# Select stage: a batch's output rows are spread in two halves inside the next batch's score groups, and its first scores stand around the output projection

## The chip, the cores and the metric

One core of a Trainium2 chip runs the whole program. The metric is the device time of one execution in microseconds (us). TensorE (PE) multiplies matrices into PSUM, which has eight banks; VectorE (DVE) and ScalarE (ACT) read PSUM and work on tiles in SBUF; SyncE (SP) issues the DMAs. Each engine works through its own list of instructions in order and waits for semaphores that the others raise.

## What is computed

The reference is a chain of four layers over x of shape (8, 512, 256), all in float32: a mixer, a layer of experts, a delta-rule attention, and last the layer that the change touches. Of each batch's 512 tokens that layer keeps the 256 with the largest gate, lets these attend to one another with 16 heads of 16, and adds the result, times the gate, to the kept tokens:

```python
x = x + _L1_ffn_ref(_layernorm(x, axis=-1), ...)

def _L1_ffn_ref(token_inputs, Wg, Wq, Wk, Wv, Wo):
    B, N, D = token_inputs.shape          # 8, 512, 256
    C = int(N * 0.5); H = 16; dh = 16
    gate = jax.nn.sigmoid((token_inputs @ Wg)[..., 0])
    _, idx = jax.lax.top_k(gate, C)
    attn_in = jnp.take_along_axis(token_inputs, idx[..., None], axis=1)
    q, k, v = (attn_in @ W reshaped to (B, C, H, dh) for Wq, Wk, Wv)
    scores = jnp.einsum('bqhd,bkhd->bhqk', q, k) / jnp.sqrt(jnp.float32(dh))
    attn = jax.nn.softmax(scores, axis=-1)
    o = jnp.einsum('bhqk,bkhd->bqhd', attn, v).reshape(B, C, D) @ Wo
    gate_sel = jnp.take_along_axis(gate, idx, axis=1)
    out = jnp.zeros_like(token_inputs)
    return out.at[jnp.arange(B)[:, None], idx].set(o * gate_sel[..., None])
```

## The kernel before

The four layers are four stages one after the other; `stage_select` is the last, and the change lies in it alone. It runs eight batches in a pipeline of two. A loop over steps (a, b) does the attention of batch a and, between its parts, the gate, the selection and the projections of batch b = a + 1. In the first step there is only b = 0, in the last only a = 7, so there are seven joint steps. The order on each engine is written out by hand, and nothing but the order of the calls in the loops and the waits in the functions decides it.

On TensorE a joint step is, by the names of its functions and the lines that the profile gives their matmuls:

- `scores(a, 0)` (L2161): the scores of heads 0 to 3, in two halves, into banks 0, 1 and 2, 3. VectorE takes the largest of each row (`maxima`, L2396), one instruction for each half.
- `turn_h(b)` (L2199): the normed tokens of batch b turned, into banks 6 and 7; ScalarE copies them to `hT` (L2332).
- `max_rows(a, 0)` (L2170): the maxima turned into bank 4; VectorE adds them to q (`add_max`, L2401, writes `q2`).
- `gate(b)` (L2205), then `scores_turned(a, 0)` (L2178), then `gate_column(b)` (L2211). ScalarE takes the sigmoid (L2334, with a table load before and after it) and then the exponentials (L2324). VectorE copies the gate's column (L2421) and compares it with all gates, two tiles of 128 tokens by two instructions each (`ranks(b, 0, 2)`, L2406 and L2407).
- `scores(a, 1)`, `max_rows(a, 1)`, `scores_turned(a, 1)`, `values(a, 0)` (L2188), `scores(a, 2)`. Meanwhile VectorE does `maxima(a, 1)`, `add_max(a, 1)`, `ranks(b, 2, 4)`, the sum `rank` (L2428) and `psel` (L2432), the matrix of zeros and ones that picks the rows.
- `select(b)` (L2218), which needs `psel`, and `turn_select`; groups 2 and 3 of the heads; the projections of q, k (L2234) and v (L2242) of batch b; `turn_back(a)` (L2250).
- the tail: `turn_out(a)` (L2257, bank 2), `project_out(a)` (L2264, bank 3), each behind a wait for ScalarE's copy of the one before (`OT`, L2357, and `o2`, L2359), and `spread_back(a)` (L2272), eight matmuls that put the 256 rows back to their 512 places in banks 4 and 5. VectorE multiplies these by the gate, adds the tokens and writes `outb` (L2458, four instructions), then raises `fin`.

Batch b's own `scores(b, 0)` opens the next step, so it stands on TensorE behind `spread_back(a)`, and VectorE's first `maxima` of the next step stand behind the four instructions of `outb`. `max_rows(a, 0)` waits for `fin`, since it writes bank 4. SyncE waits for `fin`, issues the store of `outb` and then the load of `xin` for three batches on (L2139, L2141). `layer_norm(b + 1)` on VectorE stands ahead of `turn_back`'s reader, late in the step. The program opens the next step's work with these two functions on TensorE:

```python
for a, b in steps:
    if a is not None:
        scores(a, 0)
    if b is not None:
        turn_h(b)
    if a is not None:
        max_rows(a, 0)
```

Of the kernel before, what the change touches and what calls it, by code (L numbers as in the profile page):

```python
# [10 lines left out]
ALU = mybir.AluOpType  # L11
# [2053 lines left out]
def stage_select(nc, io, x_in, x_out):  # L2065
# [9 lines left out]
    with ctx:  # L2075
# [17 lines left out]
        gcol = sb("gcol", [P, 2, TT])  # L2093
# [23 lines left out]
                 "sp mx mtp q2 stp ex val ox otp on oTp oT o2p o2 outp fin dvA dvB dvC").split()  # L2117
# [7 lines left out]
        rows = lambda i: slice(i * PAD, (i + 1) * PAD)  # L2125

# [18 lines left out]
        def _(pe):  # L2145
# [3 lines left out]
            def scores(a, n):  # L2149
                if n == 0:  # L2150
                    pe.wait_ge(s["kT"], 2 * a + 2)
                    if a:
                        pe.wait_ge(s["on"], a)
                        pe.wait_ge(s["oT"], a)
                        pe.wait_ge(s["o2"], a)
                for half in (0, 1):
                    if n:
                        pe.wait_ge(s["ex"], a * PAIRS + 2 * n - 1 + half)
                    for j in range(ST_):
                        for i in (2 * half, 2 * half + 1):  # L2160
                            m = pe.matmul(ps[:, i, j * SEL:(j + 1) * SEL], qT[rows(i), a % 2, n, j * P:(j + 1) * P], kT[rows(i), a % 2, n, :],  # L2161
                                          start=True, stop=True, skip_group_check=True)
                    m.then_inc(s["sp"], 1)
# [104 lines left out]
            def spread_back(a):  # L2268
                pe.wait_ge(s["o2"], a + 1)
                for t in range(TT):  # L2270
                    for j in range(ST_):
                        m = pe.matmul(ps[:, 4 + t // 2, t % 2 * DIM:(t % 2 + 1) * DIM], pselT[:, a % 2, j, t * P:(t + 1) * P], o2[:, j, :],  # L2272
                                      start=(j == 0), stop=(j == ST_ - 1))
                m.then_inc(s["outp"], 1)

            for a, b in steps:
                if a is not None:
                    scores(a, 0)
                if b is not None:
                    turn_h(b)  # L2280
                if a is not None:
# [7 lines left out]
                if a is not None:  # L2289
                    scores(a, 1), max_rows(a, 1), scores_turned(a, 1), values(a, 0), scores(a, 2)  # L2290
# [20 lines left out]
                if a is not None:  # L2311
                    turn_out(a), project_out(a), spread_back(a)
# [55 lines left out]
        def _(dve):  # L2368
# [4 lines left out]
            fin = Chain(dve, s["dvC"], 1)  # L2373
# [29 lines left out]
            def ranks(b, t0, t1):  # L2403
                g = gcol[:, b % 2, :]
# [8 lines left out]

            layer_norm(0)
            for a, b in steps:
                if a is not None:
                    maxima(a, 0), add_max(a, 0)
                if b is not None:
                    place.start(b)
                    dve.wait_ge(s["gcp"], b + 1)  # L2420
                    dve.tensor_copy(gcol[:, b % 2, :], ps[:, 7, :].rearrange("p (t c) -> p t c", c=P)[:, :, 0]).then_inc(s["gc"], 1)  # L2421
# [23 lines left out]
                if a is not None:  # L2445
                    fin.start(a)
                    dve.wait_ge(s["otp"], a + 1)
                    both = ps[:, 0:2, :].rearrange("p j (h x) -> p j h x", x=PAD)
                    fin(dve.reciprocal(rec[:, :, :], both[:, :, :, DH]))
# [4 lines left out]
                    dve.wait_ge(s["outp"], a + 1)  # L2454
                    if a:
                        dve.wait_ge(s["stored"], 16 * a)
                    for t in range(TT):
                        m = dve.scalar_tensor_tensor(out=outb[:, t, :], in0=ps[:, 4 + t // 2, t % 2 * DIM:(t % 2 + 1) * DIM],  # L2458
                                                     scalar=gcol[:, a % 2, t:t + 1], in1=xin[:, a % 3, t, :], op0=ALU.mult, op1=ALU.add)
                    m.then_inc(s["fin"], 1)  # L2460
                    fin.end()
# [101 lines left out]
```

## Time and profile before

| | us |
|---|---|
| median of 3 runs | 3530.76 |
| lowest, highest | 3529.91, 3532.61 |
| the profiled execution | 3537.61 |
| its span in the profile | 3535.8 |
| one cycle of the select stage (five alike, 3209.3 to 3482.2) | 54.6 |

The profile comes from one execution, 6.85 us longer than the median. Over the whole span TensorE is busy 83% and VectorE 67%, but the four stages have different limits. The select stage takes the last 488 us, from 3047.9 on. The page's lists by line are ruled by the other stages, so the stage is read from the chain of waits, from the instructions in order of time, and from windows on single stretches of it.

### The profile page before, as it was taken

The page shows a single profiled execution, that of the slowest core. Times are in us where ns is not written, and L with a number is a line of the kernel's source. Part 1 is how long each engine was busy: PE and PEld are TensorE (multiplying, and loading weights), DVE is VectorE, ACT ScalarE, POOL GpSimd, SP SyncE. Part 2 cuts the span into 40 slices and gives each one's busy share as a digit, 9 for nine tenths or more (in the row PEclk, how much of TensorE's full clock was granted, in tenths as well). Part 3 has the DMA queues.
Part 4 walks back from the last instruction along what each step waited for, and adds up shares of the span by engine and source line. Part 5 has one row for each costly group of instructions (what it writes and reads, how often), then busy time and mean ns, then how long its engine had stood idle before and what let it go on. Part 6 is the DMA issues. An engine that isn't in the chain of part 4 may idle for free. (4 is left out here: it accounts for less than half of the span.)

```text
span 3535.8 us, 47712 instructions
## 1 busy us (share of the span) xinstructions
PE 2945.4 (83%) x17546; PEld 2205.0 (62%) x17546; DVE 2386.3 (67%) x5793; ACT 1273.9 (36%) x2465; POOL 189.5 (5%) x181
## 2 busy tenths in 40 slices
PE   5999955988999999994579797977979787488887
PEld 2656632554699999991346576665757677355554
DVE  6877723455477777777578788788878784354542
ACT  2343311221244444441344534444453542033332
POOL 0000000003301110110000000000000000000000
PEclk8999976999999999996789999999999996599988
DMA  2000054002399999975201111111111100100000
GB/s 67 12 24 18 7 132 52 12 6 108 122 324 321 317 317 322 320 279 186 83 25 47 57 40 40 37 37 37 40 34 61 46 19 1 63 13 25 13 19 13
DMA packets 203643, 326.78 MB, mean 92 GB/s; under 512 B 37449, under 2 KB 157522, under 8 KB 202258
## 3 DMA queue, kind: packets, MB, share of 16 engines
q1 hardware_dynamic: 196930, 305.97, 26.2%
q0 software_dynamic: 6480, 17.77, 1.3%
q8 instruction: 139, 2.28, 0.3%
q14 instruction: 94, 0.77, 0.1%
HBM read 275.18 MB, written 48.50 MB: 92 GB/s over the span
## 5 line engine op out<-in xcount | busy, mean ns | idle before, releaser
L767 PE MATMUL ex_ps<-ex_xbT,ex_w 128*128 128x128 f32 x4544 | 530.6, 275 | 0.6 <-issue 0.5
L767 PEld LDWEIGHTS ex_ps<-ex_xbT,ex_w 128*128 128x128 f32 x4544 | 524.1, 192 | 4.6 <-issue 0.7
L896 ACT ACTIVATE ex_t<-ex_ps,ex_b 128x128 f32<-128x128 f32 x568 | 208.8, 368 | 334.8 <-PE ex_ps L767 307.8
L1386 PE MATMUL de_ps<-de_hT,de_w 128*128 128x512 f32 x640 | 308.2, 626 | 23.2 <-DMA de_w<-in_w_kqv_dram 18.2
L711 PE MATMUL ex_ps<-ex_xT,ex_w 128*128 128x512 f32 x512 | 230.6, 607 | 12.4 <-DVE ex_gl L1008 9.1
L1386 PEld LDWEIGHTS de_ps<-de_hT,de_w 128*128 128x128 f32 x640 | 122.5, 202 | 151.0 <-issue 143.1
L1008 DVE SCALAR_TENSOR_TENSOR ex_gl<-ex_ps,ex_b,ex_t 128x128 f32<-128x128 f32 (+1 forms) x316 | 123.6, 391 | 137.0 <-ACT ex_t L896 67.5
L711 PEld LDWEIGHTS ex_ps<-ex_xT,ex_w 128*128 128x128 f32 x512 | 98.0, 195 | 131.8 <-issue 114.9
L1583 PE MATMUL de_ps<-de_qx,de_kx 128*128 128x128 f32 x512 | 77.5, 317 | 120.9 <-ACT de_qx L1650 120.9
L1583 PEld LDWEIGHTS de_ps<-de_qx,de_kx 128*128 128x128 f32 x512 | 72.1, 226 | 142.3 <-ACT de_qx L1650 122.8
L1831 DVE SCALAR_TENSOR_TENSOR de_ya<-de_kx,de_taps,de_ya 128x512 f32<-128x512 f32 x192 | 143.5, 749 | 15.8 <-ACT de_ya L1638 11.3
L1008 DVE SCALAR_TENSOR_TENSOR ex_gm<-ex_ps,ex_b,ex_t 128x128 f32<-128x128 f32 (+1 forms) x316 | 121.6, 385 | 47.5 <-ACT ex_t L869 45.4
L177 PE MATMUL mx_ps<-mx_hT,mx_w_in 128*128 128x512 f32 x320 | 143.6, 605 | 8.3 <-ACT mx_hT L249 8.3
L1831 DVE SCALAR_TENSOR_TENSOR de_ya<-de_qx,de_taps,de_ya 128x512 f32<-128x512 f32 x192 | 141.4, 750 | 7.0 <-ACT de_ya L1638 2.2
L779 PE MATMUL ex_ps<-ex_w,ex_hid 128*128 128x256 f32 x568 | 134.5, 380 | 1.8 <-DVE ex_hid L1033 1.8
L869 ACT ACTIVATE ex_t<-ex_ps,ex_b 128x512 f32<-128x512 f32 x64 | 44.0, 687 | 207.5 <-PE ex_ps L711 191.7
L211 PE MATMUL mx_ps<-mx_h2T,mx_w_fc 128*128 128x512 f32 x256 | 113.6, 603 | 0.8 <-ACT mx_h2T L271 0.8
L1030 DVE SCALAR_TENSOR_TENSOR ex_gl<-ex_gl,ex_gm 128x128 f32<-128x128 f32 (+1 forms) x316 | 105.3, 333 | 11.1 <-DVE ex_gl L1028 0.2
L1033 DVE TENSOR_TENSOR ex_hid<-ex_gl,ex_gs 128x128 f32<-128x128 f32 (+1 forms) x316 | 104.9, 332 | 11.2
L220 PE MATMUL mx_ps<-mx_w_proj,mx_hid 128*128 128x256 f32 x512 | 111.8, 379 | 0.0
L177 PEld LDWEIGHTS mx_ps<-mx_hT,mx_w_in 128*128 128x128 f32 x320 | 60.7, 193 | 81.6 <-issue 67.4
L779 PEld LDWEIGHTS ex_ps<-ex_w,ex_hid 128*128 128x128 f32 x568 | 102.5, 190 | 12.9 <-DVE ex_hid L1033 1.9
(382 smaller groups left out, 5655.9 us busy)
## 6 DMA issues: line engine op xcount, KB each, us to landing
ex_w<-in_w_all_dram SPq DMA_DIRECT2D x144, 1024.0 KB, 6.2
ex_w<-in_w_all_dram SPq DMA_DIRECT2D x72, 512.0 KB, 8.5
de_w<-in_w_kqv_dram SPq DMA_DIRECT2D x80, 256.0 KB, 3.5
de_ab<-alpha_d SPq DMA_DIRECT2D x8, 2048.0 KB, 7.2
ex_xb<-ex_xs_d SPq DMA_DIRECT2D x71, 129.0 KB
ex_xs_d<-ex_blank SPq DMA_DIRECT2D x71, 128.5 KB, 7.9
ex_w<-ex_y_d SPq DMA_DIRECT2D x16, 512.0 KB, 6.2
mx_xin<-in_x_dram SPq DMA_DIRECT2D x8, 512.0 KB, 3.9
```

The costliest lines, as they stand in the source:

```text
L177: m = pe.matmul(ps[:, (n + 2) % 4, :], w_in[:, k, part * DIM + half * P:part * DIM + (half + 1) * P], hT[:, k, :], start=(k == 0), stop=(k ...
L211: m = pe.matmul(ps[:, 4 + f % 2, :], w_fc[:, k, f * P:(f + 1) * P], h2T[:, k, :], start=(k == 0), stop=(k == KT - 1))
L220: m = pe.matmul(ps[:, 6 + t // 2, t % 2 * DIM:(t % 2 + 1) * DIM], hid[:, f, t * P:(t + 1) * P], w_proj[:, f, :], start=(f == 0), stop=(f = ...
L711: m = pe.matmul(ps[:, bank, :], w[:, k, part * HID + c * P:part * HID + (c + 1) * P], xT[:, i % (LAG + 1), k, :], start=(k == 0), stop=(k ...
L767: m = pe.matmul(ps[:, n % 4, x * BLK:(x + 1) * BLK], w[:, k, part * HID + c * P:part * HID + (c + 1) * P], xbT[sx][:, k, :], start=(k == 0 ...
L779: m = pe.matmul(ps[:, 4 + sx, t * DIM:(t + 1) * DIM], hid[:, sx, c, t * P:(t + 1) * P], w2[s][:, c, :], start=(c == 0), stop=(c == HT - 1))
L896: act.activation(t1[:, n % 2, 0:BLK], ps[:, n % 4, 0:BLK], ACT.Identity, bias=b13[s][:, 0, n:n + 1]).then_inc(t1_ready, 1)
L1008: dve.scalar_tensor_tensor(out=out[:, 0:width], in0=in0, scalar=b3[:, 1, n:n + 1], in1=t1[:, n % 2, 0:width], op0=ALU.add, op1=ALU.mult).t ...
L1030: link2(dve.scalar_tensor_tensor(out=gl[:, 0:width], in0=gl[:, 0:width], scalar=1.0, in1=gm[:, 0:width], op0=ALU.add, op1=ALU.mult))
L1386: m = pe.matmul(ps[:, n % 2, :], w[:, g % SLOTS, k, n % 2 * P:(n % 2 + 1) * P], hT[:, k, :], start=(k == 0), stop=(k == KT - 1))
L1583: m = pe.matmul(wide(pair(c))[:, hd, :], kc(b, hd, c), qc(hd, c), start=True, stop=True, skip_group_check=True)
L1831: m = dve.scalar_tensor_tensor(out=y, in0=xp(b, n)[:, i:i + SEQ], scalar=taps[:, col_of(n), i:i + 1], in1=y, op0=ALU.mult, op1=ALU.add)
```

## The change

`spread_back` gets a second argument, the part, and does two of the four tiles in each call. For batch a - 1 both parts are done in the step of batch a, part 0 ahead of `max_rows(a, 0)` and part 1 between `scores(a, 1)` and `max_rows(a, 1)`, both into bank 5. Part 1 waits until VectorE has read part 0 (`outd`). On VectorE the four instructions that write `outb` are split in two by the new `put_back`, which follows `add_max(a, 0)` and `add_max(a, 1)`. `fin` is raised after part 1, and the wait for it moves from `max_rows(a, 0)` to `max_rows(a, 2)`, the first to write bank 5. `gcol` is kept for three batches instead of two. The last batch's two parts follow the loop, in banks 4 and 5.

`scores(b, 0)` is cut into its halves. The first stands between `turn_out(a)` and `project_out(a)` and waits for k and for `on` (banks 0 and 1 read). The second stands behind `project_out(a)` and `turn_h(b + 1)` and waits for `oT` and `o2` (banks 2 and 3 read). `turn_h(b + 1)` itself moves from the next step to this place. No arithmetic is added or left out.

```diff
+        spread_bank = lambda a, part: 4 if a == BATCH - 1 and part == 0 else 5
...
+            def first_scores(a, half):
+                if half == 0:
                     pe.wait_ge(s["kT"], 2 * a + 2)
                     if a:
                         pe.wait_ge(s["on"], a)
-                        pe.wait_ge(s["oT"], a)
-                        pe.wait_ge(s["o2"], a)
+                elif a:
+                    pe.wait_ge(s["oT"], a)
+                    pe.wait_ge(s["o2"], a)
+                score_half(a, 0, half)
...
             def max_rows(a, n):
                 pe.wait_ge(s["mx"], a * PAIRS + 2 * n + 2)
-                if n == 0 and a:
+                if n == 2 and a:
                     pe.wait_ge(s["fin"], a)
...
-            def spread_back(a):
+            def spread_back(a, part):
                 pe.wait_ge(s["o2"], a + 1)
-                for t in range(TT):
+                if part and spread_bank(a, 0) == spread_bank(a, 1):
+                    pe.wait_ge(s["outd"], a + 1)
+                for t in (2 * part, 2 * part + 1):
...
             for a, b in steps:
-                if a is not None:
-                    scores(a, 0)
-                if b is not None:
+                if a is None:
                     turn_h(b)
-                if a is not None:
+                else:
+                    if a:
+                        spread_back(a - 1, 0)
                     max_rows(a, 0)
...
-                    scores(a, 1), max_rows(a, 1), scores_turned(a, 1), values(a, 0), scores(a, 2)
+                    scores(a, 1)
+                    if a:
+                        spread_back(a - 1, 1)
+                    max_rows(a, 1), scores_turned(a, 1), values(a, 0), scores(a, 2)
...
-                    turn_out(a), project_out(a), spread_back(a)
+                    turn_out(a)
+                if b is not None:
+                    first_scores(b, 0)
+                if a is not None:
+                    project_out(a)
+                if b is not None:
+                    if b + 1 < BATCH:
+                        turn_h(b + 1)
+                    first_scores(b, 1)
+            spread_back(BATCH - 1, 0), spread_back(BATCH - 1, 1)
...
+            def put_back(a, part):
+                if part == 0:
+                    if a:
+                        dve.wait_ge(s["stored"], 16 * a)
+                dve.wait_ge(s["outp"], 2 * a + part + 1)
+                for t in (2 * part, 2 * part + 1):
+                    m = dve.scalar_tensor_tensor(out=outb[:, t, :], ...)
+                m.then_inc(s["fin"] if part else s["outd"], 1)
...
                 if a is not None:
                     maxima(a, 0), add_max(a, 0)
+                    if a:
+                        put_back(a - 1, 0)
...
                     maxima(a, 1), add_max(a, 1)
+                    if a:
+                        put_back(a - 1, 1)
```

On TensorE, from the end of the first joint step into the second, before (each row one kind of matmul in a row, the last number how many):

```order
950 L2257 MATMUL se_ps<-se_ident,se_O 128x128 x4
951 L2264 MATMUL se_ps<-se_wo,se_OT 128x256 x4
952 L2272 MATMUL se_ps<-se_o,se_pselT 128x256 x8
953 L2161 MATMUL se_ps<-se_kT,se_qT 128x256 x8
954 L2199 MATMUL se_ps<-se_ident,se_h 128x128 x8
955 L2170 MATMUL se_ps<-se_ident,se_M 128x128 x2
956 L2205 MATMUL se_ps<-se_hT,se_wg 128x512 x2
957 L2178 MATMUL se_ps<-se_q,se_kT 128x256 x8
958 L2211 MATMUL se_ps<-se_ident,se_gb 128x128 x4
959 L2161 MATMUL se_ps<-se_kT,se_qT 128x256 x8
960 L2170 MATMUL se_ps<-se_ident,se_M 128x128 x2
```

And now, where L2153 are scores, L2271 the output projection, L2206 `turn_h`, L2281 the spreading and L2177 `max_rows`:

```order
951 L2264 MATMUL se_ps<-se_ident,se_O 128x128 x4
952 L2153 MATMUL se_ps<-se_kT,se_qT 128x256 x4
953 L2271 MATMUL se_ps<-se_wo,se_OT 128x256 x4
954 L2206 MATMUL se_ps<-se_ident,se_h 128x128 x8
955 L2153 MATMUL se_ps<-se_kT,se_qT 128x256 x4
956 L2281 MATMUL se_ps<-se_o,se_pselT 128x256 x4
957 L2177 MATMUL se_ps<-se_ident,se_M 128x128 x2
958 L2212 MATMUL se_ps<-se_hT,se_wg 128x512 x2
959 L2185 MATMUL se_ps<-se_q,se_kT 128x256 x8
960 L2218 MATMUL se_ps<-se_ident,se_gb 128x128 x4
961 L2153 MATMUL se_ps<-se_kT,se_qT 128x256 x8
962 L2281 MATMUL se_ps<-se_o,se_pselT 128x256 x4
```

Four of the eight spreading matmuls are gone from in front of L2177, and stand behind the second group's scores; the first scores are now ahead of both.

On VectorE, at the end of the program, where only the last batch's attention runs, the two halves of the seventh batch stand between that batch's groups (L2417 maxima, L2422 `add_max`, L2441 `put_back`):

```order
4632 L2441 SCALAR_TENSOR_TENSOR se_outb<-se_ps,se_gcol,se_xin 128x256 x2
4633 L2417 TENSOR_REDUCE se_M<-se_ps 128x2x2 x2
4634 L2422 TENSOR_TENSOR se_q<-se_qT,se_ps 128x256
4635 L2441 SCALAR_TENSOR_TENSOR se_outb<-se_ps,se_gcol,se_xin 128x256 x2
4636 L2417 TENSOR_REDUCE se_M<-se_ps 128x2x2 x2
```

Before, all four (L2458) stood ahead of the first maxima; in a joint step the same pairs stand ahead of the gate's column and ahead of `ranks(b, 2, 4)`.

## Rows read from the trace of the kernel before

**Rows 1.** Windows on one whole cycle: length, busy time by engine, granted clock last-but-two.

```profile
core 0: us, PE busy (x) PEld busy (x) DVE busy (x) ACT busy (x) POOL busy (x), PEclk, DMA share, GB/s
3318.40:3373.00 54.60, 44.92 (x318) 30.83 (x317) 27.47 (x69) 17.82 (x21) 0.00 (x0) 0.91 0.06 20
```

**Rows 2.** The chain that ended last, tail and head of a cycle: start, length.

```profile
3364.91 2.01 PE se_ps L2264 x8
3367.59 3.73 PE se_ps L2272 x16
3371.34 1.66 DVE se_outb L2458 x4
3373.00 2.27 DVE se_M L2396 x2
...
3381.81 0.77 DVE se_cmp L2407 x2
3384.19 2.37 DVE se_M L2396 x2
...
3393.65 3.65 PE se_ps L2218 x16
```

**Rows 3.** In order of time, tail of a cycle: start, length, engine, line, idle before.

```profile
3363.57 0.60 PE L2257 MATMUL se_ps<-se_ident,se_O 128*128 128x128 f32 x4
...
3364.26 0.59 ACT L2357 ACTIVATE se_OT<-se_ps 128x512 f32<-128x512 f32 x1
...
3366.94 0.60 ACT L2359 ACTIVATE se_o<-se_ps 128x512 f32<-128x512 f32 x1 [2.08 <-PE se_ps L2264]
...
3371.24 1.16 PE L2161 MATMUL se_ps<-se_kT,se_qT 32*128 32x256 f32 x16
...
3372.33 1.09 PE L2199 MATMUL se_ps<-se_ident,se_h 128*128 128x128 f32 x8
```

**Rows 4.** In order of time, head of the cycle before, up to the next layer norm.

```profile
3320.72 0.44 PE L2170 MATMUL se_ps<-se_ident,se_M 128*128 128x128 f32 x2 [1.90 <-DVE se_M L2396]
...
3326.22 0.16 DVE L2421 COPY se_gcol<-se_ps 128x4 f32<-128x4 f32 x1 [4.61 <-PE se_ps L2211]
...
3332.00 0.69 PE L2170 MATMUL se_ps<-se_ident,se_M 128*128 128x128 f32 x2 [2.82 <-DVE se_M L2396]
...
3332.72 0.42 DVE L2401 TENSOR_TENSOR se_q<-se_qT,se_ps 128x256 f32<-128x256 f32 x1 [0.78 <-PE se_ps L2170]
3333.06 0.74 DVE L2406 TENSOR_SCALAR_CACHE_REDUCE se_cmp<-se_gb,se_gcol 128x512 f32<-128x512 f32 x1
...
3336.42 1.14 DVE L2432 TENSOR_SCALAR se_psel<-se_iota,se_rank 128x256 f32<-128x256 f32 x4
...
3338.97 3.72 PE L2218 MATMUL se_ps<-se_psel,se_h 128*128 128x256 f32 x16
...
3351.12 1.40 DVE L2379 BATCH_NORM_STATS2 se_stats<-se_xin 128x6 f32<-128x256 f32 x4
```

**Rows 5.** Windows on stretches of that cycle: the clock that TensorE was granted.

```profile
3321.60:3324.80 3.20, 3.20 (x11) 1.12 (x14) 0.01 (x1) 0.64 (x2) 0.00 (x0) 0.50 0.38 130
3328.30:3331.70 3.40, 0.88 (x8) 0.43 (x6) 3.33 (x6) 0.00 (x0) 0.00 (x0) 1.00 0.00 0
3331.80:3338.50 6.70, 5.99 (x46) 3.56 (x50) 4.80 (x15) 1.94 (x2) 0.00 (x0) 0.50 0.01 2
3338.60:3372.60 34.00, 30.50 (x226) 22.66 (x221) 14.18 (x40) 9.75 (x13) 0.00 (x0) 1.00 0.00 0
```

**Rows 6.** In order of time, the same head in the first joint step, at full clock.

```profile
3104.30 0.44 PE L2170 MATMUL se_ps<-se_ident,se_M 128*128 128x128 f32 x2 [1.41 <-DVE se_M L2396]
...
3108.17 0.16 DVE L2421 COPY se_gcol<-se_ps 128x4 f32<-128x4 f32 x1 [2.97 <-PE se_ps L2211]
```

**Rows 7.** The tile `se_xin` on SyncE's queue: time from issue to landing.

```profile
DMA to landing us min/median/max: 3.8/4.6/10.1
```

**Rows 8.** In order of time, the last step: its second `max_rows`.

```profile
3493.22 0.69 PE L2170 MATMUL se_ps<-se_ident,se_M 128*128 128x128 f32 x2 [1.55 <-DVE se_M L2396]
```

More of the change, by code:

```diff
@@ L2092, in stage_select @@
         gb = sb("gb", [P, SEQ])
-        gcol = sb("gcol", [P, 2, TT])
+        gcol = sb("gcol", [P, 3, TT])
         cmp = sb("cmp", [P, SEQ])
@@ L2147, in _, with score_half @@
             pe.wait_ge(s["zeroed"], 3)
-            def scores(a, n):
-                if n == 0:
+            def score_half(a, n, half):
+                for j in range(ST_):
+                    for i in (2 * half, 2 * half + 1):
+                        m = pe.matmul(ps[:, i, j * SEL:(j + 1) * SEL], qT[rows(i), a % 2, n, j * P:(j + 1) * P], kT[rows(i), a % 2, n, :],
+                                      start=True, stop=True, skip_group_check=True)
+                m.then_inc(s["sp"], 1)
+            def first_scores(a, half):
+                if half == 0:
                     pe.wait_ge(s["kT"], 2 * a + 2)
@@ L2153, in scores @@
                         pe.wait_ge(s["on"], a)
-                        pe.wait_ge(s["oT"], a)
-                        pe.wait_ge(s["o2"], a)
-                for half in (0, 1):
[L2157 to L2163, printed above, removed]
+                elif a:
+                    pe.wait_ge(s["oT"], a)
+                    pe.wait_ge(s["o2"], a)
+                score_half(a, 0, half)
+            def scores(a, n):
+                for half in (0, 1):
+                    pe.wait_ge(s["ex"], a * PAIRS + 2 * n - 1 + half)
+                    score_half(a, n, half)
             def max_rows(a, n):
                 pe.wait_ge(s["mx"], a * PAIRS + 2 * n + 2)
-                if n == 0 and a:
+                if n == 2 and a:
                     pe.wait_ge(s["fin"], a)
@@ L2372, in _ @@
             place = Chain(dve, s["dvB"], 9)
-            fin = Chain(dve, s["dvC"], 1)
+            div = Chain(dve, s["dvC"], 1)
             def layer_norm(b):
@@ L2412, in picked @@
                 dve.tensor_copy(pselT[:, b % 2, j, :], ps[:, 7 - j, :]).then_inc(s["pT"], 1)
+            def put_back(a, part):
[4 more added lines that the diff above has]
+                for t in (2 * part, 2 * part + 1):
+                    m = dve.scalar_tensor_tensor(out=outb[:, t, :], in0=ps[:, spread_bank(a, part), t % 2 * DIM:(t % 2 + 1) * DIM],
+                                                 scalar=gcol[:, a % 3, t:t + 1], in1=xin[:, a % 3, t, :], op0=ALU.mult, op1=ALU.add)
+                m.then_inc(s["fin"] if part else s["outd"], 1)
             layer_norm(0)
@@ L2453, in _ @@
                     m.then_inc(s["on"], 1)
[L2454 to L2461, printed above, removed]
+                    div.end()
+            put_back(BATCH - 1, 0), put_back(BATCH - 1, 1)
     return own
```

12 lines of the change are left out of this document (6 added, 6 removed).

## The prediction

> **What bounds the kernel now.** I read the windows by cycle first, then the chain of waits, then the instructions in order of time, then windows on the clock. The page's lists by line are no help here, since the stage that changes is the last seventh of the span. A cycle of the select stage takes 54.60 us [rows 1], with TensorE busy 44.9 and VectorE 27.5. Neither is full, so the length is set by a chain that changes engines. The chain in [rows 2] shows which one. In the tail it is the output projection (3364.91), the spreading (3367.59, 3.73 us), the four instructions of `outb` on VectorE (3371.34, 1.66) and only then the first maxima (3373.00, 2.27). The scores which these maxima read were made at 3371.24 and had waited for nothing but TensorE's order [rows 3]. In the head the chain runs over the compares (L2407) to the second maxima at 3384.19, and over TensorE from there to `select` at 3393.65. Behind `select` TensorE is busy 30.5 of 34.0 us [rows 5] and is itself the bound. The change goes at the tail and touches the head.
>
> I cut the cycle at five points and ask of each piece how long it is now and how long it will be. The pieces are taken from the cycle 3318.40 to 3373.00. Its repetition is exact enough to carry points over: `outb` starts at 3371.34, and the second `max_rows` of this cycle, 3332.00, lies where the chain's maxima of the next cycle (3384.19 + 2.37 = 3386.56) place it one period of 54.60 later. So the next first `max_rows` is at 3320.72 + 54.60 = 3375.32.
>
> **Piece A, from the end of `turn_out` to the first `max_rows`.** Now: 3363.57 + 0.60 = 3364.17 [rows 3] to 3375.32, that is 11.15 us. After the change TensorE does, from 3364.17:
> - the first half of the scores, half of 1.16 us, taken as 0.55. It ends at 3364.72. ScalarE's `OT` is ready only at 3364.26 + 0.59 = 3364.85, so this half costs nothing: it fills a wait.
> - the output projection from 3364.91 as now, 1.99 us, to 3366.90.
> - `turn_h`, 1.09 us, to 3367.97. ScalarE's `o2` (3366.94 + 0.60) is done within it, so the wait of 0.7 us ahead of the spreading is covered as well.
> - the second half of the scores, 0.55, to 3368.5, and half of the spreading, 1.83 (half of 3.73 less the overlap of neighbours), to 3370.35.
> The first maxima now run beside this: the first half during the output projection, the second from 3368.5 to 3369.7 (half of 2.37). They are ready before TensorE is, so `max_rows` starts at 3370.35. The piece is 6.18 long and gives back 4.97 us. Taken apart these are the second half of the spreading, 1.83, `outb` 1.66 off the chain, and the rest of the maxima's wait.
>
> **Piece B, first `max_rows` to the gate's column.** Now 3320.72 to 3326.22, 5.50 us [rows 4]. In the first joint step the same instructions take 3104.30 to 3108.17, 3.87 us [rows 6]. The difference is the clock: from 3321.60 to 3324.80 the granted clock is 0.50, the 1.2 GHz level [rows 5], after TensorE had sat idle 1.90 us ahead of `max_rows` [rows 4]. Piece A leaves TensorE without a gap there, so I expect full clock and 1.63 us back. `put_back` of part 0 (half of 1.66, 0.83) stands on VectorE between `add_max` and the gate's column. It waits for a spreading that is already done, and VectorE was idle 4.61 us there [rows 4]. It costs nothing. Queued behind it are the column and the compares, for which TensorE's second maxima wait; the cover lasts as long as part 0 ends 2 us before the column.
>
> **Piece C, gate's column to the second `max_rows`.** Now 3326.22 to 3332.00, 5.78 us, and VectorE is busy through it (compares, then maxima). It stays. The spreading's second part goes into TensorE's wait of 2.82 us there [rows 4], and at full clock its 1.83 fits with about 1.2 us to spare, since the scores are done at about 2.75 us after the column and the maxima at 5.78. At the low clock it takes 3.65 and overshoots by some 1.2 us.
>
> **Piece D, second `max_rows` to `select`.** Now 3332.00 to 3338.97, 6.97 us, set by TensorE at clock 0.50 from 3331.80 to 3338.50 [rows 5]; `psel` was done at 3336.42 + 1.14 = 3337.56, 1.4 us earlier. Afterwards VectorE sets it: `max_rows` 0.44, `add_max` 0.42 with two hand-overs of 0.05, `put_back` of part 1 at 0.83, then compares to `psel` as now, 3333.06 to 3337.56, 4.50. Together 6.26. That gives back 0.71. Were it not for `put_back` it would give 1.5, so 0.83 of the moved work is paid here.
>
> **Piece E, `select` to the end of `turn_out`,** 3338.97 to 3364.17, 25.2 us at full clock, has nothing changed in it. The new wait for `fin` in the third group is for something finished some 7 us earlier.
>
> **SyncE.** The load of `xin` for three batches on now follows `fin` in the step in which its layer norm comes. Part 1 is put back about 1.7 us after the second `max_rows`, issue of store and load takes 0.9, the transfer lands 4.6 us later (at most 10.1) [rows 7]. The layer norm starts 3351.12 - 3332.00 = 19.1 us after that `max_rows` [rows 4]. So 12 us are left, 6 in the worst case. Cost nothing.
>
> **The clock's share.** A, B and D give 4.97 + 1.63 + 0.71 = 7.3 us, a cycle of 47.3, if TensorE keeps the full clock. It may not. In the new cycle it waits about 1.2 us ahead of the second group's scores, 1.2 ahead of the second `max_rows` and 2.2 ahead of `select`. In the trace, waits of 1.90 and 2.82 us in otherwise thin stretches (0.88 busy of 3.40, 3328.30 to 3331.70) were followed by half clock for 3.2 us or 6.7 us [rows 4, 5]. A half-clock stretch like the short one that falls on `select`, where TensorE is the bound, costs half of its length, 1.6 us. Bounds are none (0) and two in each cycle (3.2). By the nearest row, the 1.90 us wait with one short stretch behind it, I take one in each cycle and a second in a few: 2.0 us.
>
> The Trainium skill (TensorE: Matmul & The Clock Gate, HAM oscillation — how this bites in real kernels) tells of a kernel whose bursts of matmuls each start at the low clock because the engine idles between them. [...]
>
> **The sum.** Piece A occurs in seven tails. Six are as above, 6 × 4.97 = 29.8; in the last there is no `turn_h`, so the wait for `o2` shows again, while today's piece is as long: 5.4. B and D occur in six steps: 9.8 and 4.3. That is 49.3 us at full clock. The clock takes back 7 × 2.0 = 14.0. In the last step part 1 of the seventh batch stands in a wait of 1.55 us [rows 8] and needs 1.83 to 3.65; the final `outb` now overlaps the spreading by 0.83. Net a loss of 0.7. In all 34.6 us. Against the profiled execution: 3537.6 - 34.6 = 3503.0. The median of the runs lies 6.85 below the profiled execution, so 3496.
>
> **Rivals.**
> 1. The clock holds through every cycle. For it: the new cycle has fewer and shorter gaps. Against it: 2.2 us of wait ahead of `select`. Saves 50: 3481.
> 2. Two half-clock stretches in every cycle, one of them on the spreading's second part, which then overshoots and delays `max_rows`. For it: thin work from the gate's column to `select`. Saves 49.3 - 7 × 3.2 - 1.3 = 25.6: 3505.
> 3. Slower. TensorE's clock falls ahead of `select` and does not come back through piece E, where TensorE is the bound, so every microsecond at half clock costs half a microsecond. It eats the 7.3 us of a cycle once 14.6 us more are at half clock, and is slower by over 0.2% (7 us) from 16.6; at 20 us per cycle it is 3530.8 + 7 × 2.7 = 3550. Against it: in the cycle before, the clock was back within 6.8 us each time, and `select` has 3.7 us of unbroken work [rows 4, 5].
> 4. It doesn't do what it says: the maxima's second half or the new order still waits for something that I have missed, such as `put_back` holding up the column, and the tail's gain is paid in the head. Saves 0 to 7: 3528.
>
> **How the numbers follow.** Forecast (3488 to 3502) 0.62; rival 1 0.12; rival 2 0.17; rival 3 0.03; rival 4 0.03; something between 2 and 4, 0.03. The range 3484 to 3507 holds the forecast, nearly all of rival 2 and the slower edge of rival 1, about 0.8. A difference under 0.2% can't be told from none in this kernel. Faster 0.94, same 0.03, slower 0.03.
>
> **What the profile would show.** A: no `outb` ahead of the first maxima, half of the scores ahead of the output projection, TensorE without a gap over 0.3 us from `turn_out` to the gate. B: 3.9 us from `max_rows` to the column. C: still 5.8, with four spreading matmuls in it. D: 6.3, with `select` waiting for `psel`. Cycles of 47.3 to 51, and the granted clock at 0.50 for one short stretch near `select`. Wrong would be: cycles over 52, TensorE waiting for `outp`'s reader, or the layer norm waiting for its DMA.

## The result and the profile after

The changed kernel takes 3484.95 us (median of four runs, 3477.10 to 3488.47), against 3530.34 for the kernel before: a ratio of 0.9868 with a 95% interval of 0.985 to 0.9887. The forecast was 3496. The kernel is faster, as forecast, but by 45 us instead of 35.

The page of the profiled execution, which itself took 3488.47 us, begins so (engine, busy us and share, instructions):

```profile
span 3486.7 us, 47719 instructions
PE 2929.8 (84%) x17546; PEld 2202.5 (63%) x17546; DVE 2386.9 (68%) x5793; ACT 1273.2 (37%) x2465; POOL 187.2 (5%) x181
```

TensorE does the same 17546 matmuls. The windows on whole cycles, from one `select` to the next, answer to [rows 1] and, by their clock, to [rows 5]; the last one is the last step from its first `max_rows` on:

```profile
core 0: us, PE busy (x) PEld busy (x) DVE busy (x) ACT busy (x) POOL busy (x), PEclk, DMA share, GB/s
3215.23:3262.86 47.63, 42.20 (x317) 30.08 (x317) 27.48 (x69) 17.81 (x21) 0.00 (x0) 1.00 0.08 23
3358.10:3405.73 47.63, 42.20 (x316) 30.07 (x316) 27.48 (x69) 17.81 (x21) 0.00 (x0) 1.00 0.04 12
3437.59:3486.70 49.11, 33.94 (x229) 21.12 (x227) 13.20 (x21) 9.97 (x11) 0.00 (x0) 0.79 0.07 22
```

The six cycles between the second `select` and the eighth, which I call the steady ones, are all 47.6 us long, and the granted clock is 1.00 in each, where it was 0.91. VectorE's and ScalarE's work per cycle is as before (27.5 and 17.8); TensorE's busy time has fallen from 44.9 to 42.2, although it does the same matmuls, chiefly because none of them runs at half clock.

The instructions of one cycle in order of time answer to [rows 3, 4]. L2153 are scores, L2271 the output projection, L2206 `turn_h`, L2281 the spreading, L2177 `max_rows`, L2212 the gate, L2225 `select`:

```profile
3287.45 0.60 PE L2264 MATMUL se_ps<-se_ident,se_O 128*128 128x128 f32 x4
...
3287.98 1.13 PE L2153 MATMUL se_ps<-se_kT,se_qT 32*128 32x256 f32 x8
...
3289.04 2.00 PE L2271 MATMUL se_ps<-se_wo,se_OT 128*128 128x256 f32 x8
3289.16 1.23 DVE L2417 TENSOR_REDUCE se_M<-se_ps 128x4 f32<-128x1024 f32 x1 [2.09 <-PE se_ps L2153]
...
3290.87 1.04 PE L2206 MATMUL se_ps<-se_ident,se_h 128*128 128x128 f32 x8
...
3291.84 1.13 PE L2153 MATMUL se_ps<-se_kT,se_qT 32*128 32x256 f32 x8
...
3292.90 2.00 PE L2281 MATMUL se_ps<-se_o,se_pselT 128*128 128x256 f32 x8
...
3294.73 0.38 PE L2177 MATMUL se_ps<-se_ident,se_M 128*128 128x128 f32 x2
...
3294.95 1.88 PE L2212 MATMUL se_ps<-se_hT,se_wg 128*128 128x512 f32 x4
...
3298.55 0.16 DVE L2454 COPY se_gcol<-se_ps 128x4 f32<-128x4 f32 x1 [2.19 <-PE se_ps L2218]
...
3301.83 2.00 PE L2281 MATMUL se_ps<-se_o,se_pselT 128*128 128x256 f32 x8
...
3304.32 0.44 PE L2177 MATMUL se_ps<-se_ident,se_M 128*128 128x128 f32 x2 [0.50 <-DVE se_M L2417]
...
3305.14 0.87 DVE L2441 SCALAR_TENSOR_TENSOR se_outb<-se_ps,se_gcol,se_xin 128x256 f32<-128x256 f32 x2
...
3306.46 1.94 ACT L2345 ACTIVATE se_PT<-se_ps 128x1024 f32<-128x1024 f32 x2 [5.74 <-PE se_ps L2185]
...
3307.53 2.05 PE L2153 MATMUL se_ps<-se_kT,se_qT 32*128 32x256 f32 x16
...
3310.48 3.72 PE L2225 MATMUL se_ps<-se_psel,se_h 128*128 128x256 f32 x16 [0.90 <-DVE se_psel L2467]
```

TensorE goes from `turn_out` to the gate's column without a gap. The second half of the spreading stands in the wait ahead of the second `max_rows`, of which 0.50 us is left (2.82 before). `select` waits 0.90 us for `psel`.

### Where the 49 us between the two profiled executions lie

| stretch | before | after | saved |
|---|---|---|---|
| up to the first `select` (earlier stages and the first batch) | 3084.45 | 3083.11 | 1.3 |
| first `select` to the second | 36.27 | 36.86 | -0.6 |
| second `select` to the eighth, six cycles | 327.47 | 285.76 | 41.7 |
| eighth `select` to the end | 87.61 | 80.97 | 6.6 |

Before rounding the sum is 49.1, which is also the difference of the executions, 3537.61 and 3488.47.

**How the runs are compared.** The first `select` starts at another time in each profile, although nothing ahead of it differs between the kernels: from 3067 to 3090 us over the thirteen profiles. Three profiles taken on one chip, e9 to e11, already differ by 19 us there. So a run's time carries some 20 us from the earlier stages. That the execution with the profile lay 6.85 us above the median of before may come from there too, but no profile of a median run shows it. Below, besides the runs, I give **the stage**: from the start of the first `select` to the end of the span. It is 451.4 us before and 403.6 after. It is read from one execution for each kernel.

### The profile page after: what moved, and what is told of

The parts are those of the page before. It is cut to its first block and busy times, and to the rows that moved or that the text cites. A ratio compares the mean times of both kernels' runs of the same rounds, so it can differ in the third digit from the quotient of the medians.

```text
span 3486.7 us, 47719 instructions
## 1 busy us (share of the span) xinstructions
PE 2929.8 (84%) x17546; PEld 2202.5 (63%) x17546; DVE 2386.9 (68%) x5793; ACT 1273.2 (37%) x2465; POOL 187.2 (5%) x181
## 5 line engine op out<-in xcount | busy, mean ns | idle before, releaser
L1008 DVE SCALAR_TENSOR_TENSOR ex_gm<-ex_ps,ex_b,ex_t 128x128 f32<-128x128 f32 (+1 forms) x316 | 121.8, 385 | 48.1 <-ACT ex_t L869 46.8
L2417 DVE TENSOR_REDUCE se_M<-se_ps 128x4 f32<-128x1024 f32 x64 | 76.2, 1222 | 70.3 <-PE se_ps L2153 70.1
```

What stands on the lines that cost most here:

```text
L1008: dve.scalar_tensor_tensor(out=out[:, 0:width], in0=in0, scalar=b3[:, 1, n:n + 1], in1=t1[:, n % 2, 0:width], op0=ALU.add, op1=ALU.mult).t ...
L2417: dve.tensor_reduce(M[:, n, :, at].rearrange("p j i -> p i j"), ps[:, 2 * half:2 * half + 2, :].rearrange("p i (j n) -> p i j n", n=SEL), ...
```

## The experiments

My theory after the result: the pieces A, B and D of the prediction are right in mechanism and nearly in size, and the term for the clock was too high, because the changed order leaves no wait long enough. Its rival: the clock is a matter of chance in each execution, and the profiled one was lucky. Each experiment ran four to eleven times against the kernel before. e1 to e4 shared one chip and their runs of before, e5 to e8 a second and e9 to e11 a third. The columns on cycles and the stage come from one profile for each kernel.

| kernel | median | ratio to before, interval | cycles | stage |
|---|---|---|---|---|
| before | 3530.34 | | 54.6 | 451.4 |
| after | 3484.95 | 0.9868, 0.985 to 0.9887 | 47.6 | 403.6 |
| e1 after again | 3486.63 | 0.987, 0.985 to 0.9891 | 47.6 (four), 50.9, 53.1 | 410.9 |
| e2 spreading only | 3489.91 | 0.9883, 0.9866 to 0.9901 | 48.2 to 49.7 | 410.1 |
| e3 first scores only | 3519.72 | 0.9959, 0.9946 to 0.9972 | 51.6 to 53.7 | 439.3 |
| e4 second half of `outb` late | 3488.30 | 0.988, 0.9865 to 0.9896 | 46.8 to 50.7 | 407.5 |
| e5 before, with filling | 3528.80 | 0.9987, 0.9967 to 1.0007 | 53.0, then 54.5 or 54.6 | 449.0 |
| e6 part 1 late | 3505.93 | 0.9911, 0.988 to 0.9942 | 49.7 to 53.5 | 427.6 |
| e7 after, with filling | 3480.92 | 0.9841, 0.981 to 0.9873 | 47.6 | 403.0 |
| e8 late `outb`, filling, last step | 3476.85 | 0.9835, 0.9803 to 0.9866 | 46.8, one 49.8 | 396.7 |
| e9 `outb` half written twice | 3499.07 | 0.9897, 0.9867 to 0.9926 | 48.4 to 51.5 | 413.4 |
| e10 first scores not split | 3497.01 | 0.9905, 0.9875 to 0.9935 | 48.1 to 49.7 | 409.6 |
| e11 e8 with more filling | 3469.74 | 0.9818, 0.9787 to 0.985 | 46.8 | 392.0 |

### e1: the changed kernel again

> The changed kernel once more, in the same session as the next three. Theory (the waits of a cycle are now all short, so TensorE keeps the full clock in the steady cycles and no step depends on chance): six cycles of 47.6 us, granted clock 1.00 in each, time 3485 within 2 us. Rival (the clock holds in some executions and falls in others, which is why four executions lay between 3477 and 3488): at least one cycle of 49 us or more in this profile, and a scatter of 10 us again.

Median 3486.63, single runs from 3479.4 to 3505.11, so the spread is 26 us, more than either theory had. Windows on two cycles in a row, and the `select` with which the second begins:

```profile
3259.76:3307.39 47.63, 42.20 (x316) 30.03 (x316) 27.47 (x69) 17.81 (x21) 0.00 (x0) 1.00 0.07 21
3307.39:3358.25 50.86, 45.44 (x317) 31.81 (x317) 27.47 (x69) 17.81 (x21) 0.00 (x0) 0.93 0.07 23
...
3307.39 5.33 PE L2225 MATMUL se_ps<-se_psel,se_h 128*128 128x256 f32 x16 [0.90 <-DVE se_psel L2467]
```

Four cycles are as in the first profile, then the clock falls as `select` starts (5.33 us instead of 3.72) and again in the fourth group; the sixth cycle, with three such falls, takes 53.1. The rival holds in this: the same program keeps the clock in all six cycles of one execution and loses it in two of another. So the prediction's mechanism, a half-clock stretch on `select` worth 1.6 us, is real; what was wrong is how often.

### e2 and e3: either half of the change alone

e2 leaves the first scores and `turn_h` where they stood:

```diff
-                if a is None:
+                if a is not None:
+                    first_scores(a, 0), first_scores(a, 1)
+                if b is not None:
                     turn_h(b)
-                else:
+                if a is not None:
                     if a:
                         spread_back(a - 1, 0)
...
                 if a is not None:
-                    turn_out(a)
-                if b is not None:
-                    first_scores(b, 0)
-                if a is not None:
-                    project_out(a)
...
+                    turn_out(a), project_out(a)
```

> Only the spreading is moved into the next step in two halves; the first scores and the turning of h stand where they stood before, behind the output projection. Theory (the spreading and the writing of outb carry nearly all of the tail's gain, the early scores only fill two waits of 0.65 us and let the first maxima start early): the tail from the end of turn_out to max_rows is 6.9 to 7.2 us against 6.4, cycles of 48.3 to 48.5, 6 us more than the changed kernel: 3491. Rival (each half of the change gives about half): 11.15 - 2.4 = 8.8 us of tail, cycles of 50, 3503.

e3 is the kernel before with the new tail, `spread_back(a)` whole behind `first_scores(b, 1)`, and on VectorE the four instructions of `outb` behind the first `maxima`.

> Only the first scores and the turning of h are moved around the output projection; the spreading stays whole at the end of its own step, and VectorE writes outb behind the first maxima of the next batch. Theory: the tail is the projection, turn_h, half of the scores, 3.7 us of spreading and 1.66 of outb, about 9.7 us against 11.15 of before, with 1.7 us of wait ahead of max_rows, so the clock falls there as before: cycles of 53.1, time 3520. Rival (the half clock of before came from the maxima's wait, which is gone, so the full clock comes with the early scores alone): cycles of 50.5 or less, 3502.

A cycle of each, e2 first:

```profile
3120.75:3168.92 48.17, 42.01 (x318) 30.00 (x316) 27.51 (x69) 17.81 (x21) 0.00 (x0) 1.00 0.07 22
```

```profile
3273.41:3325.02 51.61, 43.41 (x319) 30.36 (x317) 27.75 (x69) 17.81 (x21) 0.00 (x0) 0.93 0.07 21
3325.02:3378.74 53.72, 45.51 (x318) 31.44 (x316) 27.54 (x68) 17.81 (x21) 0.00 (x0) 0.90 0.07 20
```

e2 comes out at 3489.91 (3491 was expected). Its cycles at full clock, two of the six, are 48.17; the other four take up to 49.7, with half-clock stretches in them. So at full clock moving the spreading gives 6.4 of the 7.0 us that a cycle has gained, and the early scores the last 0.5. e3 is at 3519.72 (3520 expected). The early scores alone give 0.9 to 3.0 us a cycle (so the two halves don't simply add up), since the 3.7 us of spreading and 1.7 of `outb` still stand ahead of `max_rows`:

```profile
3303.45 3.72 PE L2279 MATMUL se_ps<-se_o,se_pselT 128*128 128x256 f32 x16
...
3307.21 1.66 DVE L2430 SCALAR_TENSOR_TENSOR se_outb<-se_ps,se_gcol,se_xin 128x256 f32<-128x256 f32 x4 [2.42 <-PE se_ps L2279]
...
3309.02 0.41 PE L2177 MATMUL se_ps<-se_ident,se_M 128*128 128x128 f32 x2 [1.84 <-DVE se_outb L2430]
3309.26 1.88 PE L2212 MATMUL se_ps<-se_hT,se_wg 128*128 128x512 f32 x4
```

One detail went against my reason for it: the gate behind the wait of 1.84 us ran at full clock (1.88 us) in all six steady cycles, where it did not before behind 1.90 [rows 4, 5]. The tail, from the end of `turn_out` to `max_rows`, took 10.4 us instead of the 9.7 expected. The total was met, but not by the way that I gave.

### e4 and e9: what sets the start of `select`

In e4 `put_back(a - 1, 1)` stands behind `psel` instead of ahead of `ranks(b, 2, 4)`. In e9 its two instructions are done once more into an unused tile:

```diff
+                if part:
+                    for t in (2, 3):
+                        dve.scalar_tensor_tensor(out=waste[:, t - 2, :], ...)
                 for t in (2 * part, 2 * part + 1):
```

> The changed kernel with the second half of outb written behind psel instead of ahead of the compares. Theory (VectorE sets select's start, by the 0.90 us that TensorE waits for psel): select starts 0.87 to 0.90 us earlier in each of six cycles, the third group's maxima have slack for it, cycles of 46.8, 5 us less than the changed kernel: 3480. Rival (TensorE itself or the exponentials would be next at once): cycles of 47.3 or more, 3483.

> The changed kernel with the two instructions that write the second half of outb done twice, the first time into a tile that nobody reads, ahead of the compares that lead to psel: 0.87 us more on VectorE in each step, nothing left out. Theory (psel sets select's start, and the wait ahead of it is near the edge for the clock): select moves by 0.87 us in each of six cycles, to 48.5 us at full clock, and a half-clock stretch comes into some of them; stage from the first select to the end 409 to 418 us, against 403.6 and 410.9 in two profiles of the changed kernel. Rival (psel has slack): cycles of 47.6, stage 403 to 411.

At full clock both do what was expected: a cycle is 46.84 in e4 and 48.41 in e9, 0.79 less and 0.78 more than 47.63. So the moment at which VectorE has `psel` sets the start of `select`. But neither keeps the full clock; for e9 that was expected, and its stage, 413.4, lies in the range given. Two cycles of e4 (first two rows), then two of e9:

```profile
3116.04:3162.88 46.84, 42.19 (x318) 30.01 (x316) 26.84 (x67) 17.81 (x21) 0.00 (x0) 1.00 0.00 1
3257.49:3308.23 50.74, 46.60 (x316) 32.82 (x316) 27.45 (x69) 17.81 (x21) 0.00 (x0) 0.90 0.07 22
```

```profile
3126.79:3175.20 48.41, 42.20 (x319) 30.04 (x317) 28.39 (x71) 17.81 (x21) 0.00 (x0) 1.00 0.07 21
3276.69:3328.10 51.41, 45.21 (x317) 32.15 (x317) 28.25 (x71) 17.81 (x21) 0.00 (x0) 0.93 0.07 22
```

e4 was expected at 3480 and is at 3488.30, no faster than the changed kernel: two cycles gained 0.8 each, the next ones lost up to 3.9 to the clock, twice with the spreading's second part at half clock, the place that rival 2 of the prediction named. One of the two:

```profile
3299.46 3.62 PE L2281 MATMUL se_ps<-se_o,se_pselT 128*128 128x256 f32 x8
3302.92 0.38 PE L2177 MATMUL se_ps<-se_ident,se_M 128*128 128x128 f32 x2
```

### e5: useless matmuls in the kernel before

Four matmuls (as the spreading's second part) ahead of the second `max_rows`, into bank 5, which nobody reads until it is overwritten; nothing else is touched.

> The kernel before, with four matmuls more per step whose result nobody reads (the shape of the spreading's second part, into bank 5), put into TensorE's wait of 2.82 us ahead of the second max_rows. Nothing is moved or left out. Theory (the second half-clock stretch of a cycle, 6.8 us, follows from that thin wait, and half of the path there is TensorE's): the stretch is gone, select starts as soon as psel is there, 5.4 us after max_rows instead of 6.97, so 1.5 us less in each of seven cycles: 3522. Rival (the clock follows the total of work and not that gap, or the added matmuls delay max_rows): cycles of 54.6 or more, 3532 or more.

In order of time, one cycle of it:

```profile
3322.13 1.99 PE L2279 MATMUL se_ps<-se_o,se_pselT 128*128 128x256 f32 x8
3325.26 0.44 PE L2170 MATMUL se_ps<-se_ident,se_M 128*128 128x128 f32 x2 [1.14 <-DVE se_M L2405]
3326.21 1.16 PE L2178 MATMUL se_ps<-se_q,se_kT 32*128 32x256 f32 x16 [0.51 <-DVE se_q L2410]
...
3330.64 3.72 PE L2218 MATMUL se_ps<-se_psel,se_h 128*128 128x256 f32 x16
...
3342.32 2.11 PE L2178 MATMUL se_ps<-se_q,se_kT 32*128 32x256 f32 x16 [0.51 <-DVE se_q L2410]
```

The named stretch went exactly as the theory said: `select` follows the second `max_rows` by 5.38 us instead of 6.97, so work that nobody needs saved 1.6 us. But the cycle is 54.5, not 53. The clock now falls 12 us later, in the fourth group (L2178 in 2.11 us instead of 1.16, granted clock 0.50 from 3342.4 to 3345.6), and takes it back. The first steady cycle shows the two apart: with no fall in its fourth group it took the 53.0 that the theory gives. The ratio of 0.9987 can't be told from none. Both theories failed by half: the gap does decide over that stretch, and the gain was given back elsewhere.

### e6: the spreading's second part out of the thin stretch

`spread_back(a - 1, 1)` stands behind `scores(a, 2)`, and `put_back(a - 1, 1)` behind `psel`.

> The changed kernel with the spreading's second part, and its half of outb, moved out of the wait ahead of the second max_rows to a place directly ahead of select. Theory (part 1 is also what fills the thin stretch and keeps the clock up): the work itself moves select by 1.0 us, and a half-clock stretch comes back in most cycles, cycles near 50.5, time 3500. Rival (the full clock comes from the tail alone): cycles of 48.6 at granted clock 1.00, time 3492.

```profile
3361.24 0.69 PE L2177 MATMUL se_ps<-se_ident,se_M 128*128 128x128 f32 x2 [2.43 <-DVE se_M L2416]
3362.45 2.11 PE L2185 MATMUL se_ps<-se_q,se_kT 32*128 32x256 f32 x16 [0.51 <-DVE se_q L2421]
```

With the wait bare again (2.43 us), the half clock is back behind it in every steady cycle (L2177 0.69 instead of 0.44, L2185 2.11 instead of 1.16), the cycles are 49.7 to 53.5 and the time is 3505.93; 3500 was expected. The work itself is the same wherever it stands. In that wait it is nearly free, and it holds the clock for what follows. Together that is worth 3.6 us in the cycle shown (51.26 against 47.63), half of what the change brings; 1.0 of it was expected for the place alone. e6 moves `put_back` too, which by e4 gives back 0.79 at full clock, so against e4's 46.84 the place of these four matmuls costs 4.4. How that divides between the place and the clock the run does not show, since no steady cycle of e6 kept the clock.

### e7, e8, e11: filling the waits on purpose

`fill(bank, n)` issues n matmuls of the identity against a constant into a bank that is free at that place; nothing is left out. e7 adds one call, behind `gate_column(b)`:

```diff
+            def fill(bank, n):
+                for _ in range(n):
+                    pe.matmul(ps[:, bank, 0:DIM], ident[:, :], wv[:, 0, :], start=True, stop=True)
...
+                if a is not None:
+                    if a:
+                        pe.wait_ge(s["outd"], a)
+                    fill(5, 2)
                 if a is not None:
                     scores(a, 1)
```

> The changed kernel with two matmuls more per step whose result nobody reads, in TensorE's wait of 1.34 us ahead of the second group's scores. Theory (in the changed kernel the steady cycles are close to the edge, in some executions a half-clock stretch comes in and the next ones follow): with this wait filled every cycle stays at 47.6 with full clock in all executions, median 3479, all within 4 us. Rival (the scatter comes from the first and the last step or from other stages): median 3485 and a scatter of 10 us as before.

> Three edits together: the second half of outb behind psel (as in e4), the two filling matmuls of e7, and one to three filling matmuls into bank 7 in each of TensorE's waits of the last step. Theory: cycles of 46.8 at full clock in all executions, 5 us less than e7, and a last step of 41 us instead of 47: 3468. Rival (with psel off the path the steady part is still at the edge, and the last step's waits are too long to fill): 3480.

> e8 with four more small matmuls of 128 columns per step into bank 7, three ahead of the fourth group's max_rows (a wait of 0.96 us) and one behind it (0.5 us), where the profile of e8 shows the clock falling at 3209.2. Nothing is left out. Theory: cycles of 46.8 at full clock throughout, stage 393 us from the first select to the end against 396.7 of e8, median 3470 and a scatter that the other stages set. Rival (the added matmuls delay the path or the clock falls elsewhere): stage 397 us or more.

e7's runs lie between 3478.61 and 3485.94, 7.3 us apart where 4 were expected, and all its steady cycles are 47.63; half clock comes in only behind the eighth `select`, where the last step begins. With the fluctuation of the earlier stages the scatter can't prove it, and since the changed kernel itself kept the clock in one profile of two, neither can one profile. The intervals of e7 and of the changed kernel overlap. e8, at 3476.85, missed the 3468 of its theory and lies nearer to the 3480 of its rival: one steady cycle of its profile lost the clock. Two of its cycles, and the place where the second lost the clock:

```profile
3151.19:3198.03 46.84, 43.06 (x320) 30.68 (x321) 27.56 (x69) 17.81 (x21) 0.00 (x0) 1.00 0.08 24
3198.03:3247.85 49.82, 46.04 (x320) 32.23 (x321) 27.48 (x69) 17.81 (x21) 0.00 (x0) 0.93 0.07 22
...
3208.77 0.44 PE L2177 MATMUL se_ps<-se_ident,se_M 128*128 128x128 f32 x2 [0.96 <-DVE se_M L2445]
3209.72 2.11 PE L2185 MATMUL se_ps<-se_q,se_kT 32*128 32x256 f32 x16 [0.52 <-DVE se_q L2450]
```

e11 fills that wait too (three matmuls of 128 columns ahead of the fourth `max_rows`, one behind it). A steady cycle and the last step's stretch:

```profile
3295.37:3342.21 46.84, 43.95 (x328) 31.67 (x328) 27.47 (x69) 17.81 (x21) 0.00 (x0) 1.00 0.08 23
...
3420.00:3459.70 39.70, 34.66 (x269) 23.00 (x268) 13.60 (x22) 9.97 (x11) 0.00 (x0) 1.00 0.04 14
```

In this profile the clock never falls from the second `select` to the last matmul. The stage is 392.0 us, 12 less than the changed kernel's better profile and 59 less than before; the median is 3469.74 (3470 expected), the runs 3464.84 to 3473.01. Of the 12 us, 4.7 come from six cycles of 46.84 instead of 47.63, which is the late `outb` of e4 and not the filling, and the rest from the stretch behind the eighth `select` (80.97 to 73.95), whose waits are now filled. What the filling does for the steady cycles is seen against e4, which has the same late `outb` and no filling: 46.84 throughout instead of 46.8 to 50.7, and intervals of the ratio that don't meet. That e11 kept the clock where e8 lost it once rests on one profile of each. TensorE does more matmuls than before and the kernel is the fastest measured here.

### e10: the first scores in one piece

Both halves behind `project_out(a)` and `turn_h(b + 1)`.

> The changed kernel with both halves of the first scores behind the output projection and turn_h, one after the other. Theory (two halves with waits between them cost TensorE 1.06 us each, both in a row 1.16 together, so putting them apart has lost nearly what it won by filling a wait): max_rows is 0.2 to 0.4 us later, cycles of 47.9, stage 406 to 413 us from the first select to the end, 2 us more than the changed kernel. Rival (the early start of the first maxima is worth the 1.2 us of one maxima instruction): cycles of 48.8, 7 us more.

```profile
3194.61 1.99 PE L2271 MATMUL se_ps<-se_wo,se_OT 128*128 128x256 f32 x8 [0.74 <-ACT se_OT L2376]
3196.44 1.04 PE L2206 MATMUL se_ps<-se_ident,se_h 128*128 128x128 f32 x8
...
3197.41 1.16 PE L2153 MATMUL se_ps<-se_kT,se_qT 32*128 32x256 f32 x16
3198.50 1.99 PE L2281 MATMUL se_ps<-se_o,se_pselT 128*128 128x256 f32 x8
...
3201.00 0.44 PE L2177 MATMUL se_ps<-se_ident,se_M 128*128 128x128 f32 x2 [0.51 <-DVE se_M L2415]
```

Sixteen records of scores in a row take 1.16 us, in two calls of eight they take 1.13 each. So the split costs TensorE 1.1 us and fills a wait of 0.74, and what it wins is that `max_rows` no longer waits 0.51 us for the second maxima. At full clock the cycle is 48.1, 0.5 more than with the split (47.9 was expected); the rival's 48.8 is excluded. The first joint step loses more. There the first maxima come later, TensorE waits 2.43 us instead of 1.33 ahead of the first `max_rows`, and the gate behind it runs at half clock, which it does not in the changed kernel:

```profile
3102.20 0.44 PE L2177 MATMUL se_ps<-se_ident,se_M 128*128 128x128 f32 x2 [2.43 <-DVE se_M L2415]
3102.47 2.89 PE L2212 MATMUL se_ps<-se_hT,se_wg 128*128 128x512 f32 x4
```

From the first `select` to the second it is 40.6 us, against 36.9. The median, 3497.01, is higher than these differences explain, and its runs spread from 3491 to 3508; the profile's stage, 409.6, lies between the two of the changed kernel and in the range expected. How much of the median is the clock stays open.

## Why the prediction was right and where it was wrong

**The reading of the bound and the pieces** held; together the pieces gave 7.0 us a cycle at full clock, against 7.3 forecast. The four pieces of a cycle, from the rows of after above:

| piece | before | forecast | after |
|---|---|---|---|
| A, end of `turn_out` to first `max_rows` | 11.15 | 6.18 | 3294.73 - 3288.05 = 6.68 |
| B, to the gate's column | 5.50 | 3.87 | 3.82 |
| C, to the second `max_rows` | 5.78 | 5.78 | 5.77 |
| D, to `select` | 6.97 | 6.26 | 6.16 |
| cycle | 54.6 | 47.3 | 47.6 |

**A** was 0.5 us short: I took half of the 1.16 us of both halves for one half of the scores [rows 3], but a half by itself takes 1.13. The first half outlasts ScalarE's `OT` by 0.25, the second adds 0.5, and the projection and `turn_h`, which now overlap their neighbours, give 0.3 of it back.

**B** came back in full, with the clock at 1.00, and part 0 of `outb` was free, with VectorE still idle 2.19 us behind it. **C** had 0.50 us to spare instead of 1.2, again because the scores with their waits take longer than I took. **D** is VectorE's now, as forecast; e4 and e9 show the price of `put_back` there as 0.79 and 0.78 us against 0.83.

**The clock's share is the term that failed.** I took 2.0 us in each of seven cycles, 14.0 in all. For the six steady cycles that is 12.0. In the profile of after it is nothing there, in e1 3.2 and 5.5 us in the last two of them, 8.7 in all. Two steps of it were wrong. I put a wait of 2.2 us ahead of `select`; it is 0.90. I had let `scores(a, 2)` start as soon as TensorE was free, but its halves wait for the exponentials (ACT at 3306.46, the scores from 3307.53 on in 2.05 us instead of 1.16), so the rest of the wait is spread over the stretch in pieces of at most 0.6. And I took the length of the single wait that came before a fall as the measure, and each fall as due in each cycle. The runs showed that no single wait's length decides (the gate in e3, the fourth group in e5 and e8), that the long bare wait ahead of the second `max_rows` brought half clock in every steady cycle that had it (before, e3, e6) and none on `select` once it was filled in e5, and that the same program keeps the clock with the same waits in one execution and loses it in another (after and e1). The bounds, none and two stretches in each cycle (3.2 us), did not hold for a single cycle either: e1's sixth lost 5.5 us in three falls. In the profile of after, with waits of 1.34 us ahead of the second group's scores and 0.90 ahead of `select`, the clock stays at 1.00.

**The sum by its parts.** Six steady steps: forecast 6 × (7.3 - 2.0) = 31.8, measured 41.7. From the last `select` on: forecast 5.4 - 2.0 - 0.7 = 2.7, measured 6.6. There the tail gave 4.5 instead of 5.4 (the halves again), and the last step gained 2.1 (51.26 to 49.11) where I expected to lose 0.7; it ran at granted clock 0.79 instead of 0.71. The same window before:

```profile
3484.54:3535.80 51.26, 32.72 (x220) 19.53 (x220) 11.53 (x17) 9.97 (x11) 0.00 (x0) 0.71 0.04 12
```

Of this gain 2.0 us lie between its second `max_rows` and its third, 6.99 us instead of 9.01. So 10 of the 14 us by which the profiled pair beat the forecast come from the cycles, where the clock's share was 12 too high and the pieces 2, and 4 from the end, mostly from the clock as well. Part of the 10 is luck: in e1's execution the same kernel's steady cycles kept only 33.0 of the 41.7 us, and that is still more than the 31.8 forecast.

**Rival 1** (full clock, 3481) describes the profiled execution best, by what it saves against the profiled one of before: 49.1 us, 50 forecast. The medians of the changed kernel, 3485 and 3487, lie between rival 1 and the forecast. Executions that lose a stretch or two would give that, but the times alone don't show it: the profiled execution kept the clock in every steady cycle and was the slowest of its four. **Rival 2** was not seen in a steady cycle of the changed kernel, but its mechanism was, in e4 and in the changed kernel's last step, where the spreading's second part took 3.45 us at half clock. **Rivals 3 and 4** did not occur; the clock always came back, and the load of `xin` was never waited for.

## What to carry to other kernels

Where engines hand over in turns, a good place for work that another batch has ready is the wait that would otherwise pull TensorE's clock down: there four matmuls cost next to nothing, and a few microseconds later the cycle was 3.6 us longer. After such a change, read the granted clock cycle by cycle in more than one execution, since a gain on the path can be given back by a half-clock stretch somewhere else. And when only one stage is changed, measure that stage from a mark inside it, because the rest of the program may fluctuate by more than two versions differ: by some 20 us here, where the medians of e4 and of the changed kernel are 3 us apart.

## What the runs showed of the hardware

- **Matmuls of different heads share TensorE.** Scores use 32 of the 128 rows for each head. All four heads' matmuls one after the other take 1.16 us; two heads' alone take 1.13. The Trainium skill (TensorE: Matmul & The Clock Gate, Part 3: Packing small matmuls — row/col tiling) says that matmuls on different row groups overlap in the array. The rows of e10 and of after agree, and I had missed that cutting them apart gives the overlap up.
- **Useless work made the kernel faster.** e11 is e4 with matmuls added whose result nobody reads. Its stage is 392.0 us against 407.5, its ratio to before 0.9818 against 0.988; the two ran on different chips, each against its own runs of before.
- **Waits of nearly the same length did not do the same.** Ahead of `max_rows` and the gate, 1.90 us of wait were followed by half clock before the change, and 1.84 us by full clock in e3; 0.96 us in the fourth group was harmless in every joint step of after and was followed by half clock in steps of e1, e5 and e8. No single wait's length decides it; what does is not settled by these runs.
- **The earlier stages fluctuate.** The start of the first `select` ranged over 23 us in the thirteen profiles, whose programs are alike up to there; over 19 us among three on one chip.
